# A two-layer graph network and a spiking FFN on one core: opening reordered, count blocks of 16 targets in sets of two chunks

## What is computed

```python
def gnn(x, src, dst, W_self0, W_neigh0, b0, W_self1, W_neigh1, b1):   # x: 1250 x 1024
    deg_inv = 1.0 / max(segment_sum(ones, dst), 1.0)
    def layer(h, W_self, W_neigh, b):
        agg = segment_sum(h[src], dst)                                # 40000 edges
        return h @ W_self + (agg * deg_inv[:, None]) @ W_neigh + b
    return layer(relu(layer(x, W_self0, W_neigh0, b0)), W_self1, W_neigh1, b1)

x = x + gnn(layernorm(x), src, dst, ...)
y = square(relu(layernorm(x) @ W_fc.T)) @ W_proj.T                    # F = 4096
x = x + (spikes of 5 leaky steps driven by y) / 5
```

## Time and profile before

| | |
|---|---|
| time, median of 3 runs (lowest, highest) | 1681.68 us (1680.32, 1681.75) |
| the profiled execution's own time | 1678.42 us |
| its span | 1676.4 us |
| mean granted TensorE clock | 0.995 |
| TensorE busy in the span | 1620.6 us (97%) |
| VectorE, ScalarE, GpSimd busy | 911.3, 468.1, 109.1 us |

### The profile page before, as it was taken

The page is one execution under the profiler, slowest core; times in us unless marked ns, Lnnn a source line. Parts: engine busy times, 40 slices in busy tenths (PEclk is TensorE's granted clock), DMA queues, the critical chain, the costliest instruction groups (busy, mean ns, idle before and its releaser), DMA issues.

```text
span 1676.4 us, 22440 instructions
## 1 busy us (share of the span) xinstructions
PE 1620.6 (97%) x7761; PEld 1355.8 (81%) x7764; DVE 911.3 (54%) x1699; ACT 468.1 (28%) x830; POOL 109.1 (7%) x192
## 2 busy tenths in 40 slices
PE   4889999999999999999999999999999999999997
PEld 1667777788888888788898998998989888888884
DVE  7766677735511412456343443433433688888868
ACT  4433444401111200112230321311312222222348
POOL 1211145400000000001000000000001000000000
PEclk9999999999999999999999999999999999999998
DMA  4421243457542454446521220211204233333321
GB/s 149 166 101 73 92 142 126 157 194 277 221 144 99 159 191 163 173 165 204 213 81 46 75 74 26 100 50 50 100 25 150 100 113 113 113 113 111 109 94 48
DMA packets 55920, 205.38 MB, mean 123 GB/s; under 512 B 5330, under 2 KB 13852, under 8 KB 50340
## 3 DMA queue, kind: packets, MB, share of 16 engines
q1 hardware_dynamic: 53524, 191.76, 32.2%
q0 software_dynamic: 2320, 12.58, 1.9%
HBM read 153.85 MB, written 50.47 MB: 122 GB/s over the span
## 4 chain that ended last, share of the span: by engine, by line
PE 93%; DVE 3%; issue 2%; DMA 1%; ACT 1%; DVEq 0%; SPq 0%; ACTq 0%
PE bank L1358 26%; PE bank L1471 26%; PE bank L1452 25%; PE bank L1401 10%; PE bank L1304 3%; PE bank L1331 2%; DVE key_hot L943 1%; DMA fc_raw<-w_fc 1%; PE bank L1503 0%; ACT spikes L847 0%; DVE src_hot L941 0%; DMA pr_raw<-w_proj 0%; DVE stats L958 0%; DVE xt L991 0%; DMA dst_int<-dst_rows 0%
## 5 line engine op out<-in xcount | busy, mean ns | idle before, releaser
L1358 PE MATMUL bank<-w,xt 128*128 128x512 f32 x1920 | 450.2, 393 | 1.3 <-DVE w L1003 1.3
L1452 PE MATMUL bank<-x2t,fc_w 128*128 128x384 f32 (+1 forms) x2304 | 438.7, 350 | 4.2 <-ACT relu L812 4.2
L1452 PEld LDWEIGHTS bank<-x2t,fc_w 128*128 128x128 f32 x2304 | 411.7, 188 | 29.6 <-DVE fc_w L1140 3.6
L1471 PE MATMUL bank<-pr_w,hid 128*128 128x512 f32 (+1 forms) x1824 | 418.7, 390 | 0.0
L1358 PEld LDWEIGHTS bank<-w,xt 128*128 128x128 f32 x1920 | 357.5, 188 | 75.4 <-issue 1.6
L1471 PEld LDWEIGHTS bank<-pr_w,hid 128*128 128x128 f32 (+1 forms) x1824 | 338.1, 185 | 75.6
L1214 DVE TENSOR_TENSOR y<-y,bank 128x512 f32<-128x512 f32 (+1 forms) x152 | 104.2, 687 | 215.2 <-PE bank L1471 215.2
L1401 PE MATMUL bank<-z,at 128*128 128x512 f32 x800 | 188.8, 394 | 0.0
L1401 PEld LDWEIGHTS bank<-z,at 128*128 128x128 f32 x800 | 150.2, 190 | 30.7
L807 ACT ACTIVATE pr_w<-pr_raw 128x1024 fp32r<-128x1024 f32 x64 | 67.1, 1049 | 362.0 <-PE bank L1471 358.6
L1157 DVE TENSOR_TENSOR square<-relu 128x384 f32<-128x384 f32 (+1 forms) x96 | 56.9, 592 | 140.9 <-ACT relu L812 140.9
(11 more groups left out here) (127 smaller groups left out, 935.3 us busy)
## 6 DMA issues: line engine op xcount, KB each, us to landing
fc_raw<-w_fc SPq DMA_DIRECT2D x64, 512.0 KB, 4.3
pr_raw<-w_proj SPq DMA_DIRECT2D x64, 512.0 KB, 3.5
xt<-xt_dram SPq DMA_DIRECT2D x24, 1024.0 KB, 5.1
xt_dram<-xt SPq DMA_DIRECT2D x18, 1024.0 KB, 4.3
at<-at_dram SPq DMA_DIRECT2D x20, 640.0 KB, 5.4
part_dram<-rows SPq DMA_DIRECT2D x20, 512.0 KB, 4.1
rows<-part_dram SPq DMA_DIRECT2D x20, 512.0 KB, 4.5
rows<-x SPq DMA_DIRECT2D x18, 512.0 KB, 4.9
```

Source lines behind the costliest of these rows:

```text
L1358: ins = nc.tensor.matmul(bank[:, 2 * (u % 2) + q, :], xt[j][:, a, k, :], w[:, k, b, q * HALF:(q + 1) * HALF], start=(k == 0 and m == 0), s ...
L1452: ins = nc.tensor.matmul(bank[:, 4 + (c if g == 0 else j % 2), 0:n], fc_w[:, j % 2, k, a, :], x2t[g][:, k, v, c0:c0 + n], start=(k == 0 an ...
L1471: ins = nc.tensor.matmul(bank[0:height, 2 * (n % 2) + q, :], hid_of(g, j)[:, a, n * T:n * T + height], pr_of(j)[:, v, q * HALF:(q + 1) * H ...
```

## The change

- The window becomes a block of 16 targets, 80 in all, with 160 columns of counts; a set has two chunks. Blocks are made in an order that begins at block 56 and wraps (`FIRST_WINDOW`, `window_of`), so that the thick low targets come in S0. `BLOCK_SLOTS` places them: 1 in tile 1 of A0 (k = 6), 3 in each of tiles 2 to 8 (k = 2, 4, 6), 1 in tile 9 (k = 2); in S0 3 in tile 0 (k = 5, 6, 7), 7 in each of tiles 1 to 6 (k = 0 to 6), 6 in tiles 7 and 8 (k = 0 to 5).
- `counts_tile` has two tiles, each with its own semaphore of stores.
- The opening: dense tile 0 runs while the weight arrives; the work on chunk ranges is spread between the weight's low parts, no count block stands in it, and `POOL_LOW` is k = 5 and 6. The largest number of groups that hold one target is found from the groups' least targets (80x80 products) and no longer from all 1280.
- The queue: x row 0 and the first W tile are issued ahead of the edges.
- At G1 the first W_fc tile's parts are made after row 1 (ScalarE) and after aggregate 2 (VectorE); the first W_proj tile's load waits for the last aggregate but one.

The diff, cut to its core:

```diff
-WINDOW = 32
+WINDOW = 16
+SHIFT = 4
+FIRST_WINDOW = 7 * PER_TILE
+COUNT_TILES = 2
-SET = 3
+SET = 2
...
-WINDOW_SLOTS = {A0 + n: [(5, n)] for n in range(1, TILES)}
+for _unit, _ks in (
+        [(A0 + 1, (6,))] + [(A0 + n, (2, 4, 6)) for n in range(2, TILES - 1)] + [(A0 + 9, (2,)), (S0, (5, 6, 7))]
+        + [(S0 + p, range(7)) for p in range(1, 7)] + [(S0 + p, range(6)) for p in (7, 8)]):
...
+            load_x(0)
+            load_w(0, 0)
             for i, columns in enumerate((src_cols, dst_cols)):
...
+            sp.wait_ge(pair_done, 2 * (G1 + TILES - 1))
+            load_pr(0, 0, 0, after_first=False)
             sp.wait_ge(pair_done, 2 * (G1 + TILES))
-            load_pr(0, 0, 0, after_first=False)
             load_pr(1, 1, 1, after_first=False)
...
@@ scalar
             standard_deviation(0, 0)
-            standard_deviation(0, 1)
-            high_of_row(0, 0, ACT.Copy)
-            for k in range(2):
-                high_of_w(0, k)
...
+            high_of_w(0, 0)
+            high_of_row(0, 0, ACT.Copy)
+            for k in range(1, 6):
+                high_of_w(0, k)
+            standard_deviation(0, 1)
+            high_of_w(0, 6)
+            high_of_w(0, 7)
+            high_of_row(0, 1, ACT.Copy)
...
@@ vector
+            extent_of_chunks()
             norm_x(0)
+            chunks_of_windows()
+            low_of_row(0, 0)
+            for k in range(2):
+                low_of_w(0, k)
+            bounds_of_windows()
+            for k in range(2, POOL_LOW[0]):
+                low_of_w(0, k)
             norm_x(1)
+            low_of_w(0, KD - 1)
+            low_of_row(0, 1)
+            keys_and_ranges()
+            groups_of_targets()
+            norm_x(2)
+            most_groups()
...
+            block_of_edges(0)
...
-            low_of_fc(0, 0)
             for n in range(TILES):
                 if n >= 1:
                     low_of_row(2, n - 1)
                 take_aggregate(1, n)
+                if n == 2:
+                    low_of_fc(0, 0)
...
@@ tensor
+            dense(A0, 0, {1: turn_bounds, 3: spread_bounds, 6: lambda: turn_row(0, 1)})
+            for n in range(1, TILES):
+                between = {k: (lambda i=i: block_of_edges(i)) for k, i in BLOCK_SLOTS.get(A0 + n, [])}
                 if n + 1 < TILES:
-                    between[1] = lambda: turn_row(0, n + 1)
+                    between[4 if n == 1 else 1] = lambda: turn_row(0, n + 1)
```

More of the change, by code:

```diff
@@ L221, in gnn_ffn @@
         range_ready = sem("range_ready")
+        min_spread = sem("min_spread")
         held_ready = sem("held_ready")
@@ L235, in gnn_ffn @@
         counts_copied = sem("counts_copied")
-        at_stored = sem("at_stored")
+        at_stored = [sem(f"at_stored{j}") for j in range(COUNT_TILES)]
         w_in = [sem(f"w_in{k}") for k in range(KD)]
@@ L435, in _ @@
                     sp.dma_start(edge_int[a:b, i, :], columns[a:b, :]).then_inc(edges_in, 16)
-            load_x(0)
+            for k in range(1, 4):
+                load_w(0, k)
             load_x(1)
-            for k in range(KD):
+            for k in range(4, KD):
                 load_w(0, k)
@@ L927, in _, with key_one_hots @@
             registers = range_registers(dve, "dve")
-            def window_of_edges(v, first, end):
-                dve.wait_ge(current_ready, v + 1)
+            def key_one_hots(i, v, first, end):
+                dve.wait_ge(current_ready, i + 1)
                 for c in range(SET):
@@ L935, in window_of_edges @@
                 with dve.Fori(first, end, LOOP_CHUNKS) as g:
-                    for i, s in enumerate(LOOP_SETS):
+                    for place, s in enumerate(LOOP_SETS):
                         dve.wait_ge(hot_used[s], visit)
                         for c in range(SET):
-                            chunk = g + (SET * i + c)
+                            chunk = g + (SET * place + c)
                             if s != ACT_SET:
@@ new lines, in _ @@
+            bounds_of_windows()
+            for k in range(2, POOL_LOW[0]):
+                low_of_w(0, k)
+            norm_x(1)
+            low_of_w(0, KD - 1)
[3 more added lines that the diff above has]
+            norm_x(2)
+            most_groups()
+            dve.wait_ge(range_ready, 1)
+            dve.wait_ge(edge_cols_ready, 2)
+            dve.wait_ge(constants, 14)
+            block_of_edges(0)
+            for n in range(1, TILES):
+                blocks = blocks_of(A0 + n)
+                low_of_z(A0, n - 1)
@@ L1364, in dense, with turn_bounds @@
                         ins.then_inc(w_used, 1)
-            turn_row(0, 0)
-            pe.wait_ge(held_ready, 1)
-            pe.wait_ge(constants, 14)
-            for b, c0, c1 in ((2, 0, HALF), (3, HALF, 2 * HALF), (5, 2 * HALF, PADDED)):
-                ins = nc.tensor.matmul(bank[0:1, b, 0:c1 - c0], ones_narrow[:, :], node_held[:, c0:c1], start=True, stop=True)
-            ins.then_inc(held_summed, 1)
-            pe.wait_ge(range_ready, 1)
-            window_of_edges(0)
-            for n in range(TILES):
-                between = {}
+            def turn_bounds():
+                pe.wait_ge(edge_steps, 12)
+                for e in range(2):
+                    nc.tensor.transpose(bank[0:WINDOWS, 5, e * GROUPS:(e + 1) * GROUPS], bounds[:, e, :],
+                                        ident[0:GROUPS, 0:GROUPS]).then_inc(bounds_turned, 1)
@@ new lines, in spread_bounds @@
+            def spread_bounds():
+                pe.wait_ge(edge_steps, 13)
+                for e in range(2):
+                    c = BOUND_ROW + e * WINDOWS
+                    nc.tensor.matmul(bank[0:1, 5, c:c + WINDOWS], bound_col[:, e:e + 1], ident[0:WINDOWS, 0:WINDOWS],
+                                     start=True, stop=True).then_inc(bounds_turned, 1)
+                pe.wait_ge(many_steps, 1)
+                pe.wait_ge(constants, 14)
+                nc.tensor.matmul(bank[0:GROUPS, 5, SPREAD_AT:SPREAD_AT + GROUPS], ones_square[:, :], min_diag[:, :],
+                                 start=True, stop=True).then_inc(min_spread, 1)
@@ new lines, in sum_held @@
+            def sum_held():
+                pe.wait_ge(held_ready, 1)
+                nc.tensor.matmul(bank[0:1, 5, SPREAD_AT:SPREAD_AT + GROUPS], ones_narrow[:, :], held[:, :],
+                                 start=True, stop=True).then_inc(held_summed, 1)
+            pe.wait_ge(constants, 4)
+            turn_row(0, 0)
+            dense(A0, 0, {1: turn_bounds, 3: spread_bounds, 6: lambda: turn_row(0, 1)})
+            for n in range(1, TILES):
+                between = {k: (lambda i=i: block_of_edges(i)) for k, i in BLOCK_SLOTS.get(A0 + n, [])}
@@ L1385, in _ @@
             for p in range(TILES):
-                dense(S0, p, {k: (lambda v=v: window_of_edges(v)) for k, v in WINDOW_SLOTS.get(S0 + p, [])})
+                dense(S0, p, {k: (lambda i=i: block_of_edges(i)) for k, i in BLOCK_SLOTS.get(S0 + p, [])})
             def degree(n):
```

332 lines of the change are left out of this document (168 added, 164 removed).

## The result

| | before | after |
|---|---|---|
| median of 5 runs (lowest, highest) | 1681.52 us (1679.96, 1681.75) | 1673.79 us (1672.17, 1675.66) |
| profiled execution, its span | 1678.42, 1676.4 us | 1674.6, 1672.8 us |
| mean granted clock | 0.995 | 0.988 |

The ratio is 0.9957, interval 0.9942 to 0.9971: **7.2 us faster**, where 18.9 was forecast. The time lies in the stated range and the direction is right, but 11.7 us of the gain didn't come. The two profiled executions are only 3.8 us apart: the one of before is among its quicker ones (55 later executions took 1676 to 1682).

A forecast was written before the change was run, and what follows sets the result against it. TensorE was taken as the bound nearly everywhere. Opening and A0 -49.9, S0 +37.8 and G1 -6.8 sum to -18.9 us, from a median of 1681.7 to 1662.8 us, range 1648 to 1680.

The forecast's parts named there:

- The opening and A0: First dense matmul at 16.1 us, tile 0 done at 33.1, A0 at 152.0 against 201.9: 49.9 us earlier.
- G1: At the second aggregate, the 3.94 us wait and the half-clock slowness behind it go: 6.8 us less.
- S0: Dense work, 57 blocks, repeated loops and waits take 187.9 us against 150.1: 37.8 us longer.
- The clock: Rival: TensorE's clock falls in block 24's nine passes, slower passes and a restart, total 1667.5 us; chance 0.25.
- Loops that run again: In S0's blocks 24 to 36, 21 passes over one per block at 1.34 us each: 28.1 us.
- Tile 0: S0's first tile: VectorE's starting addition together with W's last low part costs 1.3 us.
- Blocks one k step apart: In S0, GpSimd's chain sets 2.3 us between one-pass blocks, a 0.37 us wait in 38 pairs: 14.1 us.
- The addition at each tile's start: VectorE's 1.2 us take_self addition in S0, mostly covered by a k step: 0.4 us for each of 8 tiles.
- The rest: W_proj's load can't start sooner and the second counts tile removes no wait seen in S0: nothing gained.
- That the helpers keep up: Rival: in S0 GpSimd's chain is hidden, blocks come at 1.93 us, take_self is free: 18.6 less, 1644; chance 0.12.
- That it would be slower: Rival: intervals between blocks in S0 above 2.8 us make the kernel slower, 1689 at intervals of 3.0; chance 0.08.
- That the opening ends at 45: Rival: TensorE idles in tile 0 for W 6 and row 1, ending at 45, not 33: 1675 us; chance 0.06.

The follow-up runs named there:

- The two filled runs: The changed kernel with three further 512-column matmuls at the start, or two at the end, of every pass of blocks 24 to 26: ratios 0.9958 and 0.9945.
- the earlier load: SyncE's load of the fourth hidden weight tile issued ahead of the last x2 store: ratio 0.9938 in the changed kernel, 0.9974 in the kernel before.
- Two versions: Changed kernel, fourth hidden weight load earlier, filling matmuls in thick blocks; one with blocks of 32 targets (0.9882), one without blocks in S0's first tile (0.9897).

## Why the prediction came out as it did

**The opening and A0: right.** The first dense matmul came at 15.3 (16.1), tile 0 ended at 31.6 (33.1), A0 at 152.2 (152.0). That the last is right to 0.2 us is luck: tile 0 ended 1.5 early (TensorE waited only until 28.7 for GpSimd's low part of W 6, not until 30.3), and the nine tiles behind it took 120.6 and not 118.9. The prediction also said that this was an advance and not a gain, and the run with the wide blocks shows how little of it is one: with the opening 31 us earlier and the blocks of before, G0 starts at 347.9 and not at 351.8.

**G1: right.** 6.8 us in the profile; undone by itself, 6.9 by the ratios and 6.3 in its profile.

**S0: the step that failed**, 187.9 forecast and 200.3 measured, past the 200 that the prediction gave as a sign of being wrong. Its sum put the clock and ScalarE at nothing, and took the first return of a loop for as cheap as the later ones. Of its terms:

- *The clock* was a rival at 0.25 and should have been the forecast. The two filled runs show the cause, the second of them the size: 4.9 in the profile of the changed kernel, up to 7 in others. The rival's 4.7 lies near by some luck: its parts, 2.2 for passes and 1.5 to 3 for one restart, were in truth 3.7 for three k steps at the lower level (2.77, 2.77 and 2.60 in place of 1.49) and about 1.2 for passes. What misled was window 1, where TensorE was as idle as this and kept its clock: four passes there, nine here. The Trainium skill, named beside that rival, has two cases on its page. "HAM oscillation" is that of a loop whose bursts of matmuls each wait for a transfer; the waits in block 24 were of 0.55 to 0.67 us, so it isn't this one. The short idle spells that the prediction speaks of are the page's next section (TensorE: Matmul & The Clock Gate, "A second HAM failure mode: psum-queue depth-cycling"), where TensorE often idles for a moment between groups of matmuls and the clock goes up and down. The traces agree with that one: all eight profiles of the new opening without filling show the fall in the thick blocks.
- *Loops that run again.* 1.34 was right for the later passes (1.28 at full clock), but the second pass of a block costs 1.72 (2.17 us for such a block, 0.45 for one of a single pass): in a single pass all one-hots lie ready, and the second is the first that waits, for VectorE and then for ScalarE. 11 blocks x 0.38, less 0.6 on the ten later passes, are 3.6 us. The 2.01 of the earlier trace rows was read between two passes deep in a loop, and carried to loops of two. The trace of the kernel before held the better number: window 3, with two passes, goes from 103.01 to 106.82, 3.81 us against 1.24 for a window of one, so its second pass cost 2.57.

```profile
103.01 0.85 PE bank L1304 x6
...
106.25 0.57 PE bank L1304 x3
106.82 5.34 PE bank L1358 x23
```

- *Tile 0.* Block 23 began at 160.4, 1.4 late, and was 0.9 too long; 1.3 of this was in the sum. That leaves 1.0 us. The run without blocks in tile 0 gives it back by its profile.
- *Blocks one k step apart.* 2.31 to 2.34 measured, 2.3 forecast, and a tile of seven such blocks 17.4 to 17.6 us. But blocks 42, 56, 70 and 76 wait for ScalarE, whose register load follows its copy: intervals of 3.32, 3.14, 2.80 and 3.10, 3.0 us over. Nothing in the sum stood for that engine. It is also what stands behind GpSimd, not VectorE. The 3.0 us are read from the trace; no run takes them away. The addition at each tile's start was put at 0.4, and the two intervals at it (2.16 and 2.64) are 0.1 over two usual ones.

4.9 + 3.6 + 1.0 + 3.0 = 12.5, for the 12.4. The agreement is closer than the terms are known: the clock's share differs by 2 us between executions, and small parts of either sign are left out.

**The rest: wrong by 2.2 us in the profiles.** "Nothing" was right for the load of W_proj. The 2.2 are the clock's (48 matmuls in 11.04 for 8.56) behind a pause that was there before; the nine profiled kernels with the new opening and without the earlier load took 40.0 to 41.4 us here. Of the kernel before only one execution was profiled, and by its mean clock it is one of those that lost least; by the clocks of the others the 2.2 may be no difference between the kernels at all.

**The sum.** -49.7 + 50.2 - 6.8 + 2.2 + 0.4 is -3.7, the profiles' -3.6. The rest up to 7.2 is how the two profiled executions lie among their runs: that of before 3.1 us under its median of five, that of the change 0.8 over its own.

**The rivals.** That the helpers keep up fell at the intervals of 2.33. That it would be slower needed intervals of over 2.8 throughout: only those four blocks have such. That the opening ends at 45 fell too, at 31.6; its 1675 is nearest to the measured 1673.8 by coincidence. The clock's rival, 1667.5, is the one whose mechanism came.

## What to carry over

An idle TensorE costs twice where its clock falls: a loop in which it only waits for helpers is to be priced with the matmuls behind it at half speed, and a matmul or two in the wait is cheap if it ends before the operands come (passes of 1.28 us as before) and dear if it doesn't (1.28 and 1.62 in turn). A price read deep in a loop isn't the price of the first return (1.28 and 1.72 us here); the profile before had loops of that short kind to read it from. And before an engine's work is moved from a stage where it was hidden (window 0 in the opening) to one where TensorE is the bound, the advance of the first has to be netted against what it costs there.

## What the runs showed of the hardware

- Passes of 1.28 us with four short matmuls in each brought the granted clock from 1.00 to 0.50, and two more matmuls of 512 columns in each pass kept it at 1.00.
- Behind the wait of tile 0 in S0 the clock fell in three profiles (k steps of 2.77, 2.54 and 2.47 us) and didn't in the changed kernel's (1.49), with the same code up to there.
- The pause at the FFN (3.3 to 3.5 us without a matmul) is followed by a clock of 1.00 in the profile of before and of 0.50 in that of the changed kernel, so one execution doesn't tell what a pause costs. Over 55 executions of the kernel before the mean clock runs from 0.991 to 0.995, and the median times at 0.992 and at 0.995 are those 3.8 us apart.
- Two versions have a clock of 1.00 from 20 to 1640 us in their profiles and 0.996 or 0.997 in every run. Their times lie within 0.9 and 2.2 us, over four runs each, against 3.5 us over five for the changed kernel.
